# Two MoE passes around linear attention on one core: first expert's gate and up products from raw float32 weights, second expert's halves made first

## The reference, cut to what matters

```python
def _L0_ffn_ref(hidden_states, Wg, Wu, Wd):          # 8 experts, E = 128, F = 512
    x = hidden_states.reshape(-1, H)
    def expert_step(acc, w):
        wg, wu, wd = w
        h = jax.nn.silu(x @ wg) * (x @ wu)
        return (acc + h @ wd, None)
    ...
x = L0_attn_x                                        # 8 x 1024 x 128, float32
x = x + 0.5 * _L0_ffn_ref(_layernorm(x, axis=-1), Wg, Wu, Wd)
x = x + _L0_attn_ref(_layernorm(x, axis=-1), Wq, Wk, Wv, Wo, bo)
x = x + 0.5 * _L0_ffn_ref(_layernorm(x, axis=-1), Wg, Wu, Wd)
```

## Time and profile before

| | us |
|---|---|
| median of 3 runs (lowest to highest) | 2056.73 (2056.58 to 2057.06) |
| span of the profiled execution | 2054.4 |
| PE busy | 2047.3 |
| DVE busy | 1662.1 |
| ACT busy | 1439.1 |
| POOL busy | 694.2 |

### The profile page before, as it was taken

How to read it: one execution, slowest core, us unless ns; L and a number is a source line. 1 busy time by engine, 2 the same in 40 slices (tenths; PEclk the granted TensorE clock), 3 DMA queues, 4 the chain that set the end, 5 groups by cost and what they waited for, 6 DMA issues and landing times.

```text
span 2054.4 us, 29536 instructions
## 1 busy us (share of the span) xinstructions
PE 2047.3 (100%) x9514; PEld 933.1 (45%) x9514; DVE 1662.1 (81%) x2734; ACT 1439.1 (70%) x2511; POOL 694.2 (34%) x706
## 2 busy tenths in 40 slices
PE   9999999999999999999999999999999999999999
PEld 5444444444444444444444444444444444444444
DVE  8887787888887878788888787978787878877776
ACT  7877767766776676677766776676677766666665
POOL 6511134334423432345244323442344244410000
PEclk9999999999999999999999999999999999999999
DMA  7111256244733542555245335453454346421100
GB/s 215 16 22 20 62 109 127 59 96 88 144 81 79 116 88 73 86 122 117 66 96 116 78 77 102 92 106 89 84 124 102 93 87 136 83 36 21 21 11 16
DMA packets 242571, 172.58 MB, mean 84 GB/s; under 512 B 157424, under 2 KB 212720, under 8 KB 242416
## 3 DMA queue, kind: packets, MB, share of 16 engines
q1 hardware_dynamic: 208480, 128.48, 26.3%
q0 software_dynamic: 33936, 42.21, 12.7%
HBM read 99.09 MB, written 30.15 MB: 63 GB/s over the span
## 4 chain that ended last, share of the span: by engine, by line
PE 97%; DVE 1%; DMA 1%; issue 1%; ACT 0%; POOL 0%; SPq 0%; DVEq 0%; ACTq 0%; POOLq 0%
PE bank L670 11%; PE bank L649 11%; PE bank L666 11%; PE bank L667 11%; PE bank L630 11%; PE bank L637 10%; PE bank L631 10%; PE bank L653 10%; PE bank L650 10%; DMA xn<-half_tok 1%; PE bank L676 0%; PE bank L675 0%; PE bank L674 0%; DVE bank L970 0%; DMA arena<-in_L_ffn_Wu 0%
## 5 line engine op out<-in xcount | busy, mean ns | idle before, releaser
L768 ACT ACTIVATE silu_sb<-bank,scal 128x512 f32<-128x512 f32 x1024 | 704.4, 688 | 575.8 <-PE bank L637 568.5
L970 DVE SCALAR_TENSOR_TENSOR bank<-silu_sb,scal,bank 128x512 f32<-128x512 f32 x984 | 737.4, 749 | 371.3 <-ACT silu_sb L768 367.7
L977 DVE TENSOR_TENSOR h_lo<-bank,h_hi 128x512 f16<-128x512 f32 x984 | 673.4, 684 | 0.1
L775 ACT ACTIVATE h_hi<-bank 128x512 f16<-128x512 f32 x984 | 581.8, 591 | 4.0 <-DVE bank L970 3.9
L630 PE MATMUL bank<-xn,wg_hi 128*128 128x512 f16 x1024 | 388.1, 379 | 0.5 <-ACT wg_hi L758 0.4
L670 PE MATMUL bank<-h_hi,wd_lo 128*128 128x512 f16 x1024 | 388.1, 379 | 0.4 <-DVE wd_lo L958 0.4
L649 PE MATMUL bank<-xn,wu_hi 128*128 128x512 f16 x1024 | 388.2, 379 | 0.2
L666 PE MATMUL bank<-h_hi,wd_hi 128*128 128x512 f16 x1024 | 388.1, 379 | 0.2 <-ACT down_sb L783 0.2
L650 PE MATMUL bank<-xn,wu_hi 128*128 128x512 f16 x1024 | 388.1, 379 | 0.0
L653 PE MATMUL bank<-xn,wu_lo 128*128 128x512 f16 x1024 | 388.1, 379 | 0.0
L667 PE MATMUL bank<-h_lo,wd_hi 128*128 128x512 f16 x1024 | 388.1, 379 | 0.0
(11 more groups left out here) (144 smaller groups left out, 1367.5 us busy)
## 6 DMA issues: line engine op xcount, KB each, us to landing
arena<-rep_scratch SPq DMA_DIRECT2D x128, 512.0 KB, 6.9
arena<-arena POOLq DMA_DIRECT2D x56, 512.0 KB, 4.9
turn_scratch<-turn_sb SPq DMA_DIRECT2D x196, 64.0 KB, 1.9
x_tok<-turn_scratch POOLq DMA_DIRECT2D x49, 256.0 KB, 5.1
rep_scratch<-arena SPq DMA_DIRECT2D x16, 512.0 KB, 2.7
x_tok<-in_L_attn_x SPq DMA_DIRECT2D x16, 256.0 KB, 5.4
term_scratch<-arena SPq DMA_DIRECT2D x8, 512.0 KB, 3.3
arena<-term_scratch SPq DMA_DIRECT2D x8, 512.0 KB, 4.4
```

The lines of the kernel that those rows point to most:

```text
L768: act.activation(silu_sb[:, n % 3, :], gate_ps[n % NG][:, :], ACT.Silu, scale=unscale[G[group(n)]]).then_inc(sem("silu"), 1)
L970: dve.scalar_tensor_tensor(up_ps[n % NUP][:, :] if n >= NF else h_sb(n), silu_sb[:, n % 3, :], (h_scale if n >= N_ALL else h_first)[group(n)],
L977: dve.tensor_tensor(h_lo[:, n % NH, :], up_ps[n % NUP][:, :], h_hi[:, n % NH, :], ALU.subtract).then_inc(sem("h_lo"), 1)
```

## The change

The numbers in `LATE`, `MAXIMA` and the like are steps n. Units 0 to 3 of segment 0 (NW = 4) now take gate and up as one float32 matmul each, from the raw weights and a float32 copy of the transposed block (`x_first`), with `spread(0)` in their midst. Expert 1's halves are made ahead of the loop, expert 0's in steps 4 and 5. Of block 0, ScalarE norms the first of four tiles and VectorE the other three; VectorE makes var_eps and shift, GpSimd only the power and the low half of the block.

```diff
-    MAXIMA = [(0, "w_diag", 1), (1, "w_scale", 1), (4, "w_max", (0, 1)), (5, "w_max", (0, 2)), (6, "w_max", (0, 3)),
+    MAXIMA = [(2, "w_max", (2, 0)), (3, "w_diag", 1), (4, "w_scale", 1), (4, "w_max", (0, 1)), (5, "w_max", (0, 2)), (6, "w_max", (0, 3)),
...
-    WARM = (22, 4, 9)
-    SPREADS = [(1, 1), (11, 2), (16, 3)]
-    LATE = {("g", 1): 0, ("u", 1): 1, ("d", 0): 2, ("d", 1): 6, ...}
+    WARM = (15, 2)
+    NW = SL
+    SPREAD_IN = 2
+    EARLY = (("g", 1), ("u", 1))
+    SPREADS = [(4, 1), (11, 2), (16, 3)]
+    LATE = {("g", 0): 4, ("u", 0): 5, ("d", 0): 5, ("d", 1): 6, ...}
...
-    VECTOR_LOW.update({("g", 2): 13, ("d", 2): 18, ("d", 0): 2})
+    VECTOR_LOW.update({("g", 2): 13, ("d", 2): 18, ("d", 0): 5})
...
-    owed.update({5: 1, 6: 1, 21: 1})
+    owed.update({4: 1, 5: 2, 6: 2, 7: 1, 21: 1})
...
             def norm_T(s):
                 if s:
-                    pe.wait_ge(sem("lo_first"), 1)
+                    pe.wait_ge(sem("x_first"), 1)
+                    pe.wait_ge(sem("xn_hi"), 1)
                     pe.wait_ge(sem("norm_second"), 1)
...
+            def gate_whole(n):
+                if n == 0:
+                    pe.wait_ge(sem("x_first"), 1)
+                    pe.wait_ge(sem("w0_in0"), 16)
+                if n >= NG:
+                    pe.wait_ge(sem("silu"), n - NG + 1)
+                pe.matmul(gate_ps[n % NG][:, :], raw_g[:, cols(n, P)], x_first, start=True, stop=True).then_inc(sem("gate"), 1)
+
+            def up_whole(n):
+                if n == 0:
+                    pe.wait_ge(sem("w1_in0"), 16)
+                if n >= NUP:
+                    pe.wait_ge(sem("h"), n - NUP + 1)
+                pe.matmul(up_ps[n % NUP][:, :], raw_u[:, cols(n, P)], x_first, start=True, stop=True).then_inc(sem("up"), 1)
...
             idle(WARM[1])
-            spread(0)
-            idle(WARM[2])
-            for n in range(NG):
-                gate_high(n)
-            for n in range(NG):
-                gate_low(n)
+            for n in range(NW):
+                gate_whole(n)
+                if n == SPREAD_IN:
+                    spread(0)
+                up_whole(n)
             for n in range(FIRST, LAST):
-                if NG <= n < NU:
+                if NW <= n < NU:
                     gate_high(n)
                     gate_low(n)
-                if 0 <= n < NU:
                     up(n)
...
-            for t in range(TT):
-                norm(0, t, 0, "norm")
+            norm(0, 0, 0, "norm")
             act.wait_ge(sem("norm_T"), 1)
+            act.activation(x_first, down_ps[:, :], ACT.Copy).then_inc(sem("x_first"), 1)
             act.activation(xn_hi[:, 0, :], down_ps[:, :], ACT.Copy).then_inc(sem("xn_hi"), 1)
-            weight_high("g", wg_hi, raw_g, G, 0)
-            weight_high("u", wu_hi, raw_u, U, 0)
+            silu(0)
+            silu(1)
+            weight_high("g", wg_hi, raw_g, G, 1)
+            weight_high("u", wu_hi, raw_u, U, 1)
+            silu(2)
             for n in range(FIRST, LAST):
...
             norm_aggr(0, "stats", 1, "mean_var")
+            dve.wait_ge(sem("mean_var"), 1)
+            dve.tensor_scalar(var_eps[:, 0, :], mean_var[:, 0, :, 1], LN_EPS, None, ALU.add).then_inc(sem("var_first"), 1)
+            dve.wait_ge(sem("rstd_first"), 1)
+            dve.scalar_tensor_tensor(shift[:, 0, :], mean_var[:, 0, :, 0], -1.0, rstd[:, 0, :], ALU.mult, ALU.mult
+                                     ).then_inc(sem("shift"), 1)
+            for t in range(1, TT):
+                dve.tensor_scalar(xn_tok[:, 0, cols(t, P)], x_tok[:, t, :], mean_var[:, 0, t, 0:1], rstd[:, 0, t:t + 1],
+                                  ALU.subtract, ALU.mult).then_inc(sem("norm"), 1)
             for w in range(2):
                 piece_max(w, 0, amax_row[w])
...
-            dve.wait_ge(sem("xn_hi"), 1)
-            dve.tensor_tensor(xn_lo[:, 0, :], down_ps[:, :], xn_hi[:, 0, :], ALU.subtract).then_inc(sem("lo_first"), 1)
             weight_scale(0)
             group_scales(0)
-            weight_low("g", wg_hi, wg_lo, raw_g, G, 0)
-            weight_low("u", wu_hi, wu_lo, raw_u, U, 0)
-            piece_max(2, 0, amax_row[DN[0]])
+            h(0)
+            weight_low("g", wg_hi, wg_lo, raw_g, G, 1)
+            weight_low("u", wu_hi, wu_lo, raw_u, U, 1)
             for n in range(FIRST, LAST):
-                if 0 <= n < NU:
+                if 1 <= n < NU:
                     h(n)
...
-            row_scale(0, "", 0)
+            pool.wait_ge(sem("var_first"), 1)
+            pool.tensor_tensor(rstd[:, 0, :], var_eps[:, 0, :], minus_half[:, :], ALU.pow).then_inc(sem("rstd_first"), 1)
+            pool.wait_ge(sem("x_first"), 1)
+            pool.wait_ge(sem("xn_hi"), 1)
+            pool.tensor_tensor(xn_lo[:, 0, :], x_first, xn_hi[:, 0, :], ALU.subtract).then_inc(sem("lo_first"), 1)
             row_scale(1, "", 1)
```

More of the change, by code:

```diff
@@ L179, in macaron_program @@
             t = LATE.get((w, x), max(first_use(x) + lead, 0))
-            if x or w == "d":
+            if (w, x) not in EARLY:
                 act_at[t].append(("w" + w + "_hi", x))
@@ L467, in by_vector, with hi_count @@
         def by_vector(w, x):
-            return x == 0 and w != "d" or (w, x) in VECTOR_LOW
+            return (w, x) in EARLY or (w, x) in VECTOR_LOW
         def low_of(w, x):
             return sem(f"w{w}_lo" if by_vector(w, x) else f"w{w}_lo_pool")
+        def hi_count(x):
+            return {1: 1, 0: 2}.get(x, x + 1)
         def low_count(w, x):
@@ L621, in gate_high @@
                 i, bank = s % NX, gate_ps[n % NG]
-                if n == 0:
+                if n == NW:
                     pe.wait_ge(sem("lo_first"), 1)
                 elif c == 0:
-                    pe.wait_ge(sem("lo_first"), 2) if s == 1 else pe.wait_ge(sem(f"xn_T{i}"), 16 * (s // NX))
-                if s == 0 and c % SL == 0:
-                    pe.wait_ge(sem("wg_hi"), c // SL + 1)
+                    pe.wait_ge(sem("lo_second"), 1) if s == 1 else pe.wait_ge(sem(f"xn_T{i}"), 16 * (s // NX))
+                if s == 0 and c % SL == 0 or n == starts[1]:
+                    pe.wait_ge(sem("wg_hi"), hi_count(c // SL))
                 if n >= NG:
@@ L642, in up @@
                 i, bank = s % NX, up_ps[n % NUP]
-                if s == 0 and c % SL == 0:
-                    pe.wait_ge(sem("wu_hi"), c // SL + 1)
+                if s == 0 and c % SL == 0 or n == starts[1]:
+                    pe.wait_ge(sem("wu_hi"), hi_count(c // SL))
                 if n >= NF + NUP:
@@ L757, in weight_high @@
                 act.wait_ge(sem("w_scale"), (1, 3)[late] if w != "d" else (2, 4)[late])
+                if x == 0 and w != "d":
+                    act.wait_ge(sem("gate" if w == "g" else "up"), NW)
                 act.activation(hi[:, cols(x, FF)], raw[:, cols(x, FF)], ACT.Copy, scale=scale[of[late]]
@@ L767, in silu @@
                     act.wait_ge(sem("h"), n - 2)
-                act.activation(silu_sb[:, n % 3, :], gate_ps[n % NG][:, :], ACT.Silu, scale=unscale[G[group(n)]]
-                               ).then_inc(sem("silu"), 1)
+                act.activation(silu_sb[:, n % 3, :], gate_ps[n % NG][:, :], ACT.Silu,
+                               scale=unscale[G[group(n)]] if n >= NW else 1.0).then_inc(sem("silu"), 1)
             def high(n):
@@ L946, in group_scales @@
                 dve.wait_ge(sem("w_scale"), 1 + 2 * z)
+                if z == 0:
+                    dve.tensor_scalar(h_raw, scale[G[0]], scale[U[0]], 2.0 ** -H_EXP, ALU.mult, ALU.mult)
                 dve.tensor_scalar(h_first[z], scale[G[z]], 2.0 ** -H_EXP, None, ALU.mult)
```

17 lines of the change are left out of this document (9 added, 8 removed).

## The result

The changed kernel takes 2058.97 us (median of 21 runs, 2058.43 to 2060.34), the kernel before 2056.3 (21 runs, 2055.69 to 2057.38). The ratio is 1.0014, 95% interval [1.0008, 1.0019]: 2.7 us slower, within the 0.2% band that the prediction called no change, and still clear of noise. The span of the profiled execution went from 2054.4 to 2056.8 us.

The account below looks back on a forecast made before the run. TensorE bounds the kernel (busy 2047.3 of 2054.4 us), with VectorE and ScalarE nearly full where changed. Start -4.32, work +2.18, new waits +6.51, old waits -0.62 give 3.75; less 0.5 credit, +3.3: 2060.0 us, range 2056.5 to 2063.0.

Parts of the forecast that it names:

- Start: TensorE's first product needs only the transposed block, so it starts at 8.78 us instead of 13.10, 4.32 us earlier.
- TensorE's work: 24 float16 matmuls go (-5.17 us), eight float32 products (+6.90) and the scale's spread (+0.45) come: +2.18 us.
- Rival 2: Float32 products of 512 columns cost half, 0.43 us, moving the chain earlier: +1.1 us, 2057.8; chance 0.08.
- Wait for h(0): TensorE reaches up(3) at 15.26 us, needs h(0)'s bank and goes at 16.12: wait 0.86 us.
- Wait for diagonal 1: At spread(1), TensorE waits for VectorE's diagonal from 18.74 to 21.76 us: 3.02 us.
- Rival 3: The waits don't arise, since VectorE reaches diagonal 1 by 18.7 us: 2054.0; chance 0.04.
- Wait for the down high half: At down(0), TensorE waits from 24.67 to 26.64 us for ScalarE's last item of step 5: 1.97 us.
- Gate of unit 9: TensorE reaches this product at 33.12 us instead of 29.36 before, +3.76 us.
- The clock: TensorE's lower clock level costs about 2.05 us per slow stretch; the sum says the new waits don't bring it back.
- Rival 1: Clock falls in the wait for diagonal 1, slowing units 5 and 6: +3.4 to +5.3 us, up to 2062.0; chance 0.20.
- Credit later: Behind 33 us, earlier waits shrink because VectorE lags less than TensorE: 0.5 us credited (0 to 0.8).
- Rival 4: VectorE's norms run at twice 0.24 us beside GpSimd, first product at 9.5: 2060.7; chance 0.08.

Follow-up runs that it names:

- e3: Changed kernel with the down maximum moved into VectorE's idle time ahead of scale 0: 2059.2 us, ratio 1.0013.
- e7: Changed kernel with e3's early down maximum, diagonal 1 in VectorE's step 1, e6's ScalarE order, first down product one step later, no fillers: 2056.46 us.
- e2: Changed kernel with twelve unused float32 products filling TensorE's wait ahead of spread 1: 2058.53 us, ratio 1.0012.
- e6: e2 plus the down high half moved to the front of ScalarE's step 5: 2057.16 us, ratio 1.0001.
- e11: Changed kernel timed again without edit, on the chip of e9 and e12: 2058.37 us, ratio 1.0009.
- e4: Changed kernel with block 0 normed as before the change (row scale on GpSimd, four tiles on ScalarE): 2060.09 us, ratio 1.0018.
- e5: e3 plus unused float32 products in all three waits (spread 1, down high half, its low half): 2057.66 us, ratio 1.0004.
- e9: e8 with the first down products one step later still: 2055.89 us, ratio 0.9996.
- e8: e7 plus the spread of scale 0 one float32 pair earlier: 2055.83 us, ratio 0.9996.
- e12: e8 measured a second time without edit, on the other chip: 2055.7 us, ratio 0.9995.
- e1: Changed kernel with the spread of scale 0 one float32 pair earlier: 2058.5 us, ratio 1.0010.

## Why the prediction was right, point by point

The time lay in the range and on the forecast's side: +2.7 us against +3.3 forecast, 2058.97 against 2060.0, of which 0.4 is the kernel before itself, whose median of 21 runs is 2056.3 and not 2056.73. The path was forecast well, and the nearness of the number is in part luck: the credit below was forecast 0.7 us too small, while the clock, forecast at nothing, put some 0.4 us back into the median (by the groups, below).

- **Start.** 8.78 forecast, 8.80 in the trace, with block 0 landing 0.10 us later than before. Right.
- **TensorE's work.** 0.862 us for a float32 product of 512 columns forecast; starts at 9.77, 10.62, 11.48, 12.34 are 0.86 apart. Rival 2 (half of that) is out.
- **Wait for h(0).** 0.86 forecast; TensorE was free at 15.37 and went at 16.34, 0.97 with the hand-over. Right.
- **Wait for diagonal 1.** 18.74 to 21.76 forecast, 19.07 to 21.95 measured. Right within 0.3 us, and e3 and e7 show its cause: with the down maximum taken off VectorE's queue it shrinks to 1.60, with the diagonal early too it is gone. Rival 3 is out.
- **Wait for the down high half.** 1.97 from 24.67 forecast. The changed kernel doesn't show it, as TensorE came there at 26.6, slowed by the clock. e2 shows it: 24.74 to 26.48. e6 shows that ScalarE's order sets it.
- **Low half.** 0.66 forecast, 0.69 measured (27.06 to 27.75).
- **Gate of unit 9.** 33.12 forecast, 33.16 measured. Errors on the way cancelled: ScalarE got h(3) 0.23 us later than forecast (21.73), and took 4.09 us instead of 4.27 for the seven instructions ahead of the down high half.
- **The clock.** The step that failed: "the sum says it doesn't" (bring the low level back). It does. Rival 1 was right on the mechanism and on the hiding: the stretch is 3.3 us long, the matmuls of units 5 and 6 take 1.7 us more (26.57 - 24.87), and the wait for the down high half swallows it. That a swallowed stretch costs nothing is seen in the runs too: of the seven lowest of the changed kernel, three have a granted clock of 1.000 and four of 0.999, all within 0.21 us. The rival's price for an uncovered one was up to 2.05 us; e2's execution paid 1.54 (lag 5.34 against 3.80), or some 1.7 with its earlier first product (8.67) taken off, e3's runs 1.5. A stretch that is half covered cost 0.54 (e11's lag, 4.34), and the median run of the changed kernel, in that middle group, lies some 0.4 us above the lowest group. The rule of the Trainium skill that the prediction cited ("TensorE: Matmul & The Clock Gate", "Why this matters for your kernels") held in kind. The granted clock behind the 2.9 us of idling was 0.52; but e3's and e4's profiled executions have waits of 1.60 and 2.7 us at the same place and 1.00 behind them. What the prediction should have done is give the covered stretch to the forecast and the uncovered one to the tail. It also misread its rows in one place: "no wait of the trace is over 0.5 us" leaves out the 0.7 us ahead of the last transposes, behind which no stream follows that could show a slower clock.
- **Credit later.** Mis-sized: 0.5 (0 to 0.8) forecast, 1.17 measured (0.49 at unit 7, 0.68 at unit 16). These are the waits of the earlier trace rows, given back since VectorE lags less than TensorE (h(6) at 28.75 instead of 26.55, 2.2 us, against 3.8). The recorded waits make 0.8 us, but by distances of starts TensorE lost 1.3 us there before (0.60, 0.60 and 0.75 us at 34.9, 54.9 and 55.8, less 0.216 each): the forecast counted them without their hand-overs. The further 0.24 at unit 412 is the chance in the execution before. The mis-sized credit is the main part of what was forecast too much.
- **Rival 4** (norms slowed by GpSimd) is out: the three norms end at 7.34.

## What to carry to other kernels

Starting an engine's stream earlier pays little if the queues that feed it don't start earlier too: here TensorE began 4.3 us sooner, but scale 0 was made 2.8 us later, and TensorE met VectorE's queue at the next thing it needed. To forecast such a change, write the three or four queues out from starts in the trace; spacings of starts, not record lengths, gave a landing within 0.1 us after 20 us of schedule, with errors of up to 0.3 us on the way. Where a new wait leaves TensorE idle, as for 1.7 to 2.9 us here, ask where a slow stretch behind it would fall and whether another wait swallows it. Filling the idle time with products that nobody reads is a cheap way to find out, if all the waits are filled (e5) and not one of them (e2). And look for a small step that only the trace before has, before crediting it to the change: 0.22 us at 842 us was one.

## What the runs showed of the hardware that I had not expected

- One stretch at the lower clock level followed short idle times: it came behind a wait of 2.9 us in the changed kernel, behind waits of 1.74 and 0.69 us in e2 with the first one filled, and behind 0.7 and 1.2 us in e9 (from starts in e2, as recorded in e9). Whether and where it comes differs from run to run of the same kernel: e3's profiled execution has waits of 1.60 and 2.02 us and no stretch, while nine of its eleven timed runs are 1.5 us longer; e4's has waits of 2.7 and 1.6 us and none either. With all three waits filled (e5) the eleven runs lie within 0.2 us; with the first filled and the other two cut to 0.36 and 0.56 us (e6), within 0.4. In e7, e8 and e12, with waits of 1.3 and 0.6 us left, three runs of eleven each have 0.999 as granted clock and are 0.4 to 0.5 us longer than the median of the others.
- Two diagonals on VectorE took 0.48 us before and 1.10 us here (9.71), beside GpSimd's subtraction (9.38 to 10.53). It cost nothing here, since VectorE waited for the spread anyway. The reverse is in e1: GpSimd's four norms took 2.86 us instead of 1.74 beside VectorE's 512-column instructions, and there TensorE paid 0.75 us for it. That the two engines disturb each other is read from which records overlap; no run was made to part them.
